# Four attention-and-feed-forward layers on one core: q and k parts laid out by feature, head 0's operands built by PE, weights loaded in earlier stages

## The reference

```python
x = x + L0_attn(layernorm(x))   # window attention, 16 heads of 8, mixed with 64 latent tokens by a gate
x = x + L0_ffn(layernorm(x))    # fp4_linear(silu(fp4_linear(x, w_gate)) * fp4_linear(x, w_up), w_down)
x = x + L1_attn(layernorm(x))   # softmax over all 2048 keys, 16 heads of 8
x = n + L1_ffn(n)               # n: x + layernorm(x); 8 experts, top 2
x = x + L2_attn(layernorm(x))   # causal, q and k normalised by head, silu
x = L2_ffn(x)                   # two local-attention layers (not touched)
x = x + L3_attn(layernorm(x))   # convolution, state space recurrence
x = x + L3_ffn(layernorm(x))    # 16 gated experts

def fp4_quant_dequant(x):       # blocks of 16 along the last dim
    scale = jnp.maximum(jnp.max(jnp.abs(xb), axis=-1, keepdims=True) / 6.0, 1e-12)
    q = _GRID[jnp.searchsorted(_MID, jnp.abs(xb / scale))] * jnp.sign(xb) * scale
```

## Time and profile before

| | |
|---|---|
| time, median of 3 runs | 3141.21 us (3139.88 to 3146.33) |
| profiled execution | 3152.78 us |
| its span, first to last instruction | 3150.1 us |
| busy, PE / DVE / ACT / POOL | 2465.9 / 1904.1 / 1562.8 / 627.4 us |
| mean granted TensorE clock | 0.871 |

### The profile page before, as it was taken

How to read it: one execution, slowest core, us unless ns; L and a number is a source line. 1 busy time by engine, 2 the same in 40 slices (tenths; PEclk the granted TensorE clock), 3 DMA queues, 4 the chain that set the end, 5 groups by cost and what they waited for, 6 DMA issues and landing times. The chain is left out here.

```text
span 3150.1 us, 43914 instructions
## 1 busy us (share of the span) xinstructions
PE 2465.9 (78%) x15538; PEld 1142.9 (36%) x15538; DVE 1904.1 (60%) x2699; ACT 1562.8 (50%) x3136; POOL 627.4 (20%) x1152
## 2 busy tenths in 40 slices
PE   2886465399999999759985999999677886775658
PEld 1443233112222222237752333332346545544523
DVE  3443564689999999221125777774476384447567
ACT  1342353168888888623331566666256356432211
POOL 2553000000000000000010121221275074203236
PEclk8776687589999999969986899998789898987779
DMA  2110000311111110020002000000110010000000
GB/s 71 57 60 11 9 1 3 75 52 42 41 39 39 41 45 24 3 55 1 1 3 55 26 19 27 27 20 10 37 34 2 1 32 2 1 6 2 1 21 14
DMA packets 54370, 79.31 MB, mean 25 GB/s; under 512 B 20819, under 2 KB 33269, under 8 KB 54154
## 3 DMA queue, kind: packets, MB, share of 16 engines
q1 hardware_dynamic: 53610, 75.40, 7.7%
q10 hardware_dynamic: 544, 1.12, 0.3%
HBM read 59.56 MB, written 10.49 MB: 22 GB/s over the span
## 5 line engine op out<-in xcount | busy, mean ns | idle before, releaser
L806 DVE TENSOR_REDUCE l1a_core_mpart<-l1a_core_psA 128x1 f32<-128x1024 f32 x512 | 601.4, 1219 | 83.1 <-PE l1a_core_psA L726 83.1
L790 ACT ACTIVATE l1a_core_prob<-l1a_core_psB 128x512 f32<-128x512 f32 x1024 | 551.2, 596 | 158.5 <-PE l1a_core_psB L739 156.7
L1117 ACT ACTIVATE l2a_core_prob<-l2a_core_psB 128x384 f32<-128x384 f32 (+3 forms) x656 | 316.0, 525 | 184.7 <-PE l2a_core_psB L1059 179.9
L1137 DVE TENSOR_REDUCE l2a_core_mpart<-l2a_core_psA 128x1 f32<-128x1024 f32 (+7 forms) x384 | 335.3, 909 | 108.3 <-PE l2a_core_psA L1044 62.0
L750 PE MATMUL l1a_core_psV<-l1a_core_prob,l1a_core_vh 128*32 128x512 f32 x2048 | 273.6, 606 | 0.1
L1075 PE MATMUL l2a_core_psV<-l2a_core_prob,l2a_core_vh 128*32 128x128 f32 (+3 forms) x1856 | 196.9, 447 | 15.2 <-ACT l2a_core_prob L1117 8.8
L739 PE MATMUL l1a_core_psB<-l1a_core_qh,l1a_core_kh 75*128 75x512 bf16 x640 | 193.7, 384 | 0.8 <-ACT l1a_core_prob L790 0.8
L1869 DVE SCALAR_TENSOR_TENSOR X<-l1e_psO,W,X 128x128 f32<-128x128 f32 x128 | 36.0, 344 | 220.7 <-PE l1e_psO L1826 220.7
L1858 ACT ACTIVATE l1e_h<-l1e_psH,l1e_b 128x512 f32<-128x512 f32 x128 | 87.9, 687 | 137.5 <-PE l1e_psH L1819 137.5
L556 DVE TENSOR_REDUCE l0a_core_mrow<-l0a_core_psA 128x4 f32<-128x1024 f32 x64 | 78.3, 1225 | 114.4 <-PE l0a_core_psA L471 114.4
L998 POOL TENSOR_SCALAR_AFFINE_SELECT l2a_core_prob<-l2a_core_prob 128x128 f32<-128x128 f32 x256 | 74.2, 294 | 359.1 <-ACT l2a_core_prob L1117 357.8
(11 more groups left out here) (672 smaller groups left out, 4519.4 us busy)
## 6 DMA issues: line engine op xcount, KB each, us to landing
l2f_tab<-in_rotary SPq DMA_DIRECT2D x32, 128.0 KB
l0a_core_qh<-qparts SPq DMA_DIRECT2D x36, 96.0 KB
l0a_core_kh<-kparts SPq DMA_DIRECT2D x12, 288.0 KB
l1a_core_qa<-qparts SPq DMA_DIRECT2D x32, 96.0 KB
l1a_core_ka<-kparts SPq DMA_DIRECT2D x16, 192.0 KB
l1a_core_qh<-qparts SPq DMA_DIRECT2D x30, 96.0 KB
l1a_core_kh<-kparts SPq DMA_DIRECT2D x10, 288.0 KB
l2a_core_qh<-qparts SPq DMA_DIRECT2D x30, 96.0 KB
```

Source lines behind the costliest of these rows:

```text
L790: nc.scalar.activation(prob[u % (2 * PER_KB)][:], psB[u % 3][:], ACT.Exp, scale=scale).then_inc(b_exped, 1)
L806: nc.vector.tensor_reduce(mpart[:, n // 2, n % 2:n % 2 + 1], psA[i % 2][:], AX.X, ALU.max).then_inc(a_freed, 1)
L1117: nc.scalar.activation(prob[n % RING][:, 0:cols], psB[n % 3][:, 0:cols], ACT.Exp, scale=scale).then_inc(b_exped, 1)
L1137: ins = nc.vector.tensor_reduce(mpart[:, place, part:part + 1], psA[i % 2][:, lo * P:hi * P], AX.X, ALU.max)
```

## The change

1. `build_constants` also loads X on SP; `load_tokens` and its barrier are gone.
2. Weights live in small outer stages and are loaded ahead: those of the fronts, of the routers and of L3's projection under the norm in front (`on_sync`), the latent and the output weights of L0 on ACT's queue at the beginning of the window core (`bulk_loads`), L1's experts likewise in the wide core, L2's output weight in the causal core, and L3's gated experts on SP in `l3p`.
3. Head 0's operand rows are made by PE: POOL writes one-hot matrices (`make_picks`), eight units of three products copy the parts' rows into place in PSUM, and ACT writes them to SBUF (`fill`). The front no longer waits for its stores; SP waits for them in the core, before head 1's load. V's bias in L0 is a product with a row of ones.
4. Both `qparts` and `kparts` are [128 features, 3, S], and operand rows run by feature. A head takes six loads (three of q and three of k) instead of four, in the wide core twelve and six instead of ten and four.
5. Window core: GAP 1 to 2, and the maxima of h+1 are issued before the rows of h+3.
6. Causal core: values and slots come after every second score unit.
7. `l0h`: four `hid` buffers; the work of neighbouring chunks is woven in another order.

The diff, cut to its core:

```diff
+def load_rows(sp, g, h, qh, kh, loaded):
+    heads = slice(h * HD, (h + 1) * HD)
+    for i in range(3):
+        rows = slice(3 * HD * i, 3 * HD * (i + 1))
+        sp.dma_start(qh[rows, :], g.qparts[heads, i:i + 1, :].broadcast_to([HD, 3, S])).then_inc(loaded, 16)
+        sp.dma_start(kh[rows, :], g.kparts[heads]).then_inc(loaded, 16)
...
+    def pick_rows(self, pe, psF, part_step):
+        pe.wait_ge(self.picks_made, self.picks)
+        for n in range(2 * NC):
+            which, c = n // 2 % 2, n // 4 * 2 + n % 2
+            pe.wait_ge(part_step[which], 4 * (n // 4 + 1))
+            if n >= 2:
+                pe.wait_ge(self.filled, n - 1)
+            for i in range(3):
+                ins = self.nc.tensor.matmul(psF[n % 2][0:self.rows, :], self.pick[:, which, i, 0:self.rows],
+                                            self.parts[which][i][0:HD, c * CH:(c + 1) * CH], start=i == 0, stop=i == 2)
+            ins.then_inc(self.picked, 1)
...
-                for i in range(3):
-                    sp.dma_start(qh[b][3 * HD * i:3 * HD * (i + 1), :], g.qparts[i:i + 1, h * HD:(h + 1) * HD, :]
-                                 .broadcast_to([3, HD, S])).then_inc(qk_loaded[b], 16)
-                sp.dma_start(kh[b][0:QK_ROWS, :], g.kparts[h:h + 1].broadcast_to([3, 3 * HD, S])).then_inc(qk_loaded[b], 16)
+                load_rows(sp, g, h, qh[b], kh[b], qk_loaded[b])
...
+            sp.wait_ge(first.stored, 16 * 12)
             load_qk(1)
...
             for h in range(H):
+                if h + 1 < H:
+                    load_m(h + 1)
                 if h + 3 < H:
                     load_qk(h + 3)
-                if h + 1 < H:
-                    load_m(h + 1)
...
                 for u in range(NB):
                     score(h, u)
+                    if u % 2 == 0 and u + 1 < NB:
+                        continue
                     while row < NT * H and NB * (row // NT) + last_unit[row % NT] + LATE <= NB * h + u:
...
-            sp.wait_ge(stored, 16 * 12)
-            sp.wait_ge(feed.filled, 16 * feed.fills)
...
-            if has_bias:
-                pool.wait_ge(w_loaded, 16 * nload)
-                pool.wait_ge(v_ready, NC)
-                nc.gpsimd.tensor_tensor(g.V[:], g.V[:], bvr[:].unsqueeze(1).broadcast_to([P, NT, P]), ALU.add).then_inc(scale_step, 1)
...
+    layernorm_transpose(nc, g, "l1a_ln", on_sync=first.load_weights)
+    attention_front(nc, g, "l1a_front", first)
+    wide_attention_core(nc, g, "l1a_core", float(1.0 / np.sqrt(np.float32(P))), first, g.l1_experts.load)
```

More of the change, by code:

```diff
@@ L100, with fill @@
+    def fill(self, act, psF):
+        act.wait_ge(self.ones_set, 1)
+        for n in range(2 * NC):
+            which, c = n // 2 % 2, n // 4 * 2 + n % 2
+            act.wait_ge(self.picked, n + 1)
+            self.nc.scalar.activation(self.operands[which][0:self.rows, c * CH:(c + 1) * CH], psF[n % 2][0:self.rows, :],
+                                      ACT.Copy).then_inc(self.filled, 1)
 class Head:
@@ L1400, in _ @@
                 nc.vector.tensor_tensor(x, x, psO[c][:], ALU.add).then_inc(added, 1)
-    st.close()
+    st.close(weights)
 NLAT = 64
@@ L1993, in _ @@
             ts = nc.vector.tensor_scalar
-            dve.wait_ge(loaded, 16 * (3 + PR))
+            dve.wait_ge(loaded, ew.count)
             def times_score(n):
@@ L2239, in l0_ffn @@
     st = Stage(nc, "l0h")
-    hid = [st.sb(f"hid{i}", [P, 4, FF]) for i in range(3)]
+    hid = [st.sb(f"hid{i}", [P, 4, FF]) for i in range(NC)]
     sg = [st.sb(f"sg{i}", [P, FF]) for i in range(2)]
```

663 lines of the change are left out of this document (380 added, 283 removed).

## The result

| | before | after |
|---|---|---|
| median of the runs | 3143.77 us (4 runs, 3139.88 to 3156.1) | 3042.27 us (4 runs, 3033.47 to 3044.84) |
| ratio of the times | | 0.9666, 95% interval 0.9631 to 0.97 |
| span of the profiled execution | 3150.1 us | 3038.2 us |
| mean granted TensorE clock | 0.871 | 0.884 |

The kernel became 101.5 us faster where 154 were forecast; 3042 lies above the range. Since every stage ends at a barrier, the time can be laid out stage by stage: I take the first instruction of each stage on PE (its weight loads included), DVE or ACT from both timelines and subtract. The rows add up to 111.2 of the 111.9 between the spans; 0.6 more lies in L2's two local-attention layers, which were not touched. The measured figure for the weights is what the other rows leave.

The account below looks back on a forecast made before the run. PE was taken as the bound (78% busy), so only stage edges and gaps could give time; 7.1 + 61 + 32.7 + 27 + 22 + 4 = 153.8 off 3152.8 gave 2999 profiled, 2988 median, range 2955 to 3025.

Parts of the forecast that it names:

- Start: Kernel start: X loads beside the constants, so the first norm starts near 12.5 instead of 19.59; −7.1 us.
- weights ahead: Stage starts: weight loads lie under earlier work, removing most of eleven PE waits totalling 89.5; −61 us.
- Head 0 by PE: Joint of front and core in L0, L1, L2: PE products replace small DMAs; −32.7 us, range 25 to 37.
- Window core: Window core: wider-spread row transfers and maxima issued first bring a head from 10.96 to 9.7; −27 us.
- 8 of these: Window core's start: 8 of PE's 10.6 us of waits for rows of heads 1 and 2 would go.
- I take a stall of 0.5 to 1: Window core: with maxima first, rows of h+3 start late, stalling each head 0.5 to 1 us.
- −3 to +3 of the slack: Window core: late-issued rows of h+3 leave −3 to +3 us of slack each head.
- rival 1: Window core keeps its pace, PE waiting for rows instead of maxima; only the start gains 8; 3007 us; chance 0.22.
- L0H: FP4 stage L0H: extra hid buffer and new order remove half of DVE's 44.9 us waits; −22, range 8 to 28.
- rival 2: L0H's new order waits elsewhere, giving 8 us and not 22; 3002 us; chance 0.13.
- Causal core: Causal core: values done for two score units at a time shorten PE's exp waits; −4 us, between −10 and +12.
- Wide core: Wide core: 18 q and k issues a head instead of 14 fit in SP's time; 0 us.

Follow-up runs that it names:

- Experiment 3: Changed kernel with L0's V bias added by POOL again instead of by one-row products on PE: 3032.41 us, ratio 0.9661.
- Experiment 11: Kernel before with GAP 2 alone in the window core, rows still before maxima, old layout: 3120.69 us, one run.
- Experiments 5 and 9: Changed kernel with rows first, V's bias on POOL, L0H's first two inputs before turns: 2985.17 us; then all inputs before the down product too: 2979.89 us.
- experiment 10: Changed kernel, maxima first and GAP 2 kept, with five row buffers so rows load one head further ahead: 2991.85 us, one run.

## Why the prediction was wrong

The direction was right, the time was not. By its own steps:

- **Start** and **weights ahead**: right, 7.1 and 61 as worked out, since they came from waits whose end each row named; the waits views of PE and DVE after the change name no load of weights. Of the cover on ACT's queue less was left than thought (below).
- **Head 0 by PE**: right in L1 and L2 (21.1 and 9.4 for 17.3 and 7.6; in seven of the nine other profiles of the new layout L1's gain is 18.4). In L0 the step that failed is the last sentence of that part: "V's bias ... goes to PE as 16 short products", set at nothing. PE's projection of V stands ahead of the picks in its list, so each microsecond there is on the path; it grew from 4 to 19 us, so that all eight units of picks came behind the last part of k, at half clock, where the forecast had four: 20.6 us instead of 5.6. Experiment 3 gives 12 us back. I had priced the removed operation and its cover, and not the one that took its place.
- **Window core**: two effects of opposite sign. The layout's gain was larger than taken: 35 us with GAP 1 (212.4 against 177.6), where "8 of these" and a head of 9.7 had both effects in one number. The order's price is what failed: "I take a stall of 0.5 to 1" was 1.8 to 2.9 in eight heads, and the clock stayed at 0.82 (0.81 before) where above 0.9 was forecast. The bounds −3 to +3 of the slack held it; the value taken stood inside them with no row for it. Between 144 and 161 the rows show what it was: idle SP until mid head, 4.4 us of issues, and 3.6 from the last issue to PE. It was rival 1, with the waits of 2 us at the first product of a head's maxima that the prediction names as a sign of being wrong, except that the stage came out 4 slower and not 8 faster. One premise is weaker than both the prediction and rival 1 took it: that a wait of 2 us lowers the clock. Experiment 11 has seven waits of 1.5 to 2.7 between 108 and 250 and a clock of 0.97, so what lets the clock fall in this stage stays open.
- **L0H**: rival 2 named it, "ACT's copies now come before the silu that DVE waits for", and its gain of 8 (measured 7.1). "I take half" of DVE's 44.9 us counted the waits that go, and not those that come: 23.4 + 21.5 + 8.0 = 52.9 became 10.5 + 13.4 + 24.2 = 48.1. Experiments 5 and 9 move waits by moving inputs and win 5.3 in all; what bounds the stage at 98 was not settled.
- **Causal core**: the sign was right and the size off by four: taken 4, measured 16.9. I counted the 8.8 for exp as partly kept and left out the 5.1 for the copy in the same row; both went, and the steady heads gave 8.5. Another 8.2 came from a shorter stretch at half clock in the last two heads, which no term of the forecast held; against experiment 11's 504.9 the changed kernel's 500.7 is 4.2 shorter.
- **Wide core**: right, 729.8 and 730.7.
- **The sum**: 3141.21 − 153.8 is 2987, not 2988; it changes nothing.

The misses of L0 (14 for its front, 31 for the window core, 15 for L0H) against 13 more in the causal core and 6 more in the joints of L1 and L2 make the 42 us by which the span's gain of 112 missed 154. Rivals 1 and 2 came true together, and the range allowed for two at once only up to 3023: with the bias no rival named it.

## What to carry to other kernels

When the order of two loads on one queue is swapped, write down for each when it can be issued and when it is needed: a load that can go at once must not stand behind one whose input is ready in mid head, unless it is issued a head earlier still (experiment 10). Cost an operation that comes in place of a hidden one on its new engine, with what stands behind it there. A wait removed from a ring of engines is worth little until the next one in the ring is looked for: in L0H 52.9 us of waits became 48.1. And before a gain is put down to waits that went, compare PE's busy time and clock in the same heads: in the causal core half of the gain was clock, and the same code ran with and without it.
